# A two-layer decoder step on one core: the scan loop's selection mask moved to PSUM, and the second self-attention half and five folds placed elsewhere

## The reference

```python
x = x + mamba(layernorm(x))              # L0: projections, depthwise convolution, scan over 64 positions, gate, W_out
x = x + cross_attention(layernorm(x), ctx)   # L0: 16 heads of 128, keys and queries RMS-normed
x = x + two_expert_ffn(layernorm(x))     # L0: each row goes to the one expert its router picks
x = x + self_attention(layernorm(x))     # L1: 16 heads of 16, causal, ALiBi bias
x = x + cross_attention(layernorm(x), ctx, mask)  # L1: 16 query heads on 8 key heads
x = x + ternary_ffn(layernorm(x))        # L1: weights rounded to -1, 0, 1, rows to 8 bits

def step(state, inp):                    # the scan inside mamba
    dA = exp(dlt * A)
    state = dA * state + (dlt * u) * Bs
    y = einsum('bgdn,bgn->bgd', state, Cs)
```

## Time and profile before

| what | value |
|---|---|
| median of three runs | 927.2 us (924.82 to 931.52) |
| the profiled execution | 926.82 us, of which 924.9 us is the span from first to last instruction |
| scan loop, first to last step | about 40.2 to 273.8 us |
| second half of L1's self-attention, up to the folds | about 634.7 to 687.6 us |
| folds of L1 | 687.6 to 707.0 us |
| cross-attention and FFN of L1 | 707.0 to 924.9 us |

### The profile page before, as it was taken

One profiled execution on the slowest core, in us unless ns is written; L12 is line 12 of the kernel. 1 busy time (PEld: TensorE's weight loads), 2 busy tenths in 40 slices (PEclk: granted clock), 3 DMA queues, 4 the chain that ended last, 5 costly groups with the idle time before them and its releaser, 6 DMA issues.

```text
span 924.9 us, 12509 instructions
## 1 busy us (share of the span) xinstructions
PE 818.7 (89%) x5082; PEld 501.8 (54%) x5082; DVE 548.1 (59%) x666; ACT 434.1 (47%) x650; POOL 302.3 (33%) x147
## 2 busy tenths in 40 slices
PE   6687797977999889999999899997989799989976
PEld 2232333322445456566666676666677566667754
DVE  3799989899994232333433452437872534464686
ACT  3764666635524555555545312233554222232475
POOL 0089999899870000000001010102009990000000
PEclk9889999899999999999999999998989999999999
DMA  9666666776994100000000031415000000000001
GB/s 301 176 172 172 185 166 172 181 182 181 249 264 157 47 1 1 1 1 1 1 1 25 27 103 57 176 44 226 2 3 1 1 1 1 1 1 1 1 1 46
DMA packets 26377, 77.02 MB, mean 83 GB/s; under 512 B 3569, under 2 KB 10481, under 8 KB 25073
## 3 DMA queue, kind: packets, MB, share of 16 engines
q1 hardware_dynamic: 25552, 74.13, 27.8%
q0 software_dynamic: 768, 2.10, 0.6%
HBM read 68.75 MB, written 7.08 MB: 82 GB/s over the span
## 4 chain that ended last, share of the span: by engine, by line
PE 54%; DVE 13%; DMA 11%; ACT 10%; POOL 6%; issue 5%; SPq 0%; POOLq 0%; DVEq 0%; ACTq 0%
PE ps L1268 11%; PE ps L1184 9%; DMA region_b<-m_rows 5%; DMA region_c<-m_rows 4%; PE ps L1231 4%; PE ps L1367 4%; PE ps L1393 4%; POOL region_c L464 3%; PE ps L1256 3%; PE ps L1189 2%; POOL region_b L464 2%; DVE region_c L1827 2%; PE ps L1073 2%; PE ps L1025 2%; PE ps L1158 2%
## 5 line engine op out<-in xcount | busy, mean ns | idle before, releaser
L464 POOL TENSOR_TENSOR region_c<-region_c,region_b 128x1024 f32<-128x1024 f32 x42 | 101.1, 2415 | 51.6 <-DMA region_b<-m_rows 45.5
L1073 PE MATMUL ps<-region_c,ident 128*128 128x512 f32 x168 | 90.7, 669 | 18.9 <-POOL region_c L464 12.1
L1827 DVE TENSOR_TENSOR_SCAN region_c<-region_c,ps 128x1024 f32<-128x1024 f32 x43 | 97.8, 2283 | 2.0 <-ACT ps L635 0.8
L485 POOL DMA_INDIRECT f_in<-xn,f_row x8 | 8.0, 996 | 275.3 <-DVE f_row L1938 273.5
L1268 PE MATMUL ps<-region_c 128*128 128x256 f32 x384 | 90.4, 381 | 0.1
L1268 PEld LDWEIGHTS ps<-region_c 128*128 128x128 f32 x384 | 72.2, 190 | 24.8 <-issue 16.3
L1904 DVE COPY region_b<-ps 128x512 f32<-128x512 f32 x32 | 21.6, 689 | 84.9 <-PE ps L1242 84.8
L1822 DVE TENSOR_TENSOR ps<-ps,region_c 128x1024 f32<-128x1024 f32 x52 | 63.2, 1215 | 8.7 <-PE ps L1061 8.5
L1073 PEld LDWEIGHTS ps<-region_c,ident 128*128 128x128 f32 x168 | 33.7, 209 | 58.5 <-issue 34.5
L1184 PE MATMUL ps<-xnT,region_a 128*128 128x512 f32 x128 | 61.5, 602 | 0.8 <-ACT region_c L703 0.8
L1184 PE MATMUL ps<-xnT,region_c 128*128 128x512 f32 x128 | 58.6, 594 | 0.7 <-ACT region_c L731 0.7
(11 more groups left out here) (246 smaller groups left out, 1640.8 us busy)
## 6 DMA issues: line engine op xcount, KB each, us to landing
region_b<-m_rows SPq DMA_DIRECT2D x43, 512.0 KB, 5.1
region_c<-m_rows SPq DMA_DIRECT2D x21, 512.0 KB, 4.9
xn<-m_brows SPq DMA_DIRECT2D x12, 512.0 KB, 4.4
region_a<-in_x_wo SPq DMA_DIRECT2D x2, 2048.0 KB, 11.5
m_rows<-region_b SPq DMA_DIRECT2D x4, 512.0 KB, 5.7
region_a<-in_x_wq SPq DMA_DIRECT2D x8, 256.0 KB, 7.2
region_b<-in_f_fc SPq DMA_DIRECT2D x1, 2048.0 KB, 7.9
region_b<-in_f_proj SPq DMA_DIRECT2D x1, 2048.0 KB, 13.2
```

Of the source, the lines that this page charges most:

```text
L464: pool.tensor_tensor(m_hc[u % 3], m_h[u % 3], m_cb[u % 3], ALU.mult).then_inc(sem("m_hc"), 1)
L1073: last = pe.matmul(ps[:, 4 + c, :], ident[:, :], m_hc[u % 3][:, c * HALF:c * HALF + HALF], start=(n == 0), stop=(n == DST - 1))
L1827: dve.tensor_tensor_scan(m_h[u % 3], m_da[u % 3].rearrange("p b t -> p (b t)"), inputs(u), 0.0, ALU.mult, ALU.add).then_inc(sem("m_scan"), 1)
```

## The change

In the scan loop: the mask lies in PSUM (pair(6)) and is written one step later (n = 8), after c_rows has emptied pair(6) and, at k = 1, after the lags; convolve stands at n = 12 and waits for select_log, and convolved at n = 13. columns("C") stands at n = 2 and 3, c_rows at n = 4, columns("x") at 5 and 6, lags at 7 and 8. du has a buffer for each group (one of them is ctxT, so ctxT is loaded in group 3), and step_inputs stands one step sooner (n = 13). The first decay of a group stands ahead of channels. In L1: SP holds the 5 MB until gather(1) has landed; ln_scale, ln_turn of the second half stand ahead of shift 2 and scores 3; five folds (EARLY) stand among the self-attention; wvo and wqk lie over the weights they come from (in region A), and the FFN's buffers take their place; the output bias is added in two halves.

```diff
+            def decay(u): ...             # L629 as before, called at n > 0 or k == 0, and below
+        EARLY = [("wqk", 0), ("wvo", 0), ("wvo", 1), ("wvo", 2), ("wvo", 3)]
@@ SP
+            sp.wait_ge(sem("f_back"), 128)
-            load(wo1, io["x1_wo"], "ld_x1")
+            load(wo1, io["x1_wo"], "ld_t")
@@ GpSimd
-                if n == DST - 2 and k < NK - 1:
+                if n == DST - 3 and k < NK - 1:
                     step_inputs(k + 1)
@@ ScalarE, loop
-                act.activation(m_below, m_e, ACT.Relu, scale=-1.0, bias=thr_col)
+                act.wait_ge(sem("m_cT"), k + 1)
+                if k == 2:
+                    act.wait_ge(sem("m_xs"), 2)
+                act.activation(pair(6), m_e, ACT.Relu, scale=-1.0, bias=thr_col)
-                    if n == 6:
+                    if n == 4:
                         c_rows(k + 1)
-                    if n == 7:
+                    if n in (7, 8) and k == 1:
+                        lags(1, (2 * n - 14, 2 * n - 13))
+                    if n == 8:
                         step_below(k + 1)
-                    if n in (9, 10) and k == 1:
-                        lags(1, (2 * n - 18, 2 * n - 17))
-                    if n == 12:
+                    if n == 13:
                         convolved(k + 1)
                     if n == DST - 1:
+                        decay(u + 1)
                         channels(k + 1)
@@ ScalarE, self-attention
+            def early_folded(m):
+                act.wait_ge(sem("x1_fold"), m + 1)
+                act.activation(fold_out(1, *EARLY[m]), ps[:, 6 + m % 2, :], ACT.Copy).then_inc(sem("x1_folded"), 1)
-                act.wait_ge(sem("ld_t"), 48)      # weight_sum
+                act.wait_ge(sem("ld_t"), 64)
@@ TensorE
+                if n == 2 and k < NK - 1:
+                    pe.wait_ge(sem("m_ax"), k + 2)
+                    columns("C", k + 1, (0,))
                 if u >= 2:
                     add_state(u - 2)
-                    if n == 11:
-                        if k != 1:
-                            pe.wait_ge(sem("m_cT"), k + 2)
+                    if n == 12:
+                        pe.wait_ge(sem("m_sel"), k + 1)
                         convolve(k + 1)
+                if i == 7:
+                    for m in range(1, 5):
+                        early_fold(m)
+                    pe.wait_ge(sem("x1_folded"), 5)
@@ VectorE
-                dve.copy_predicated(m_ln, m_below.bitcast(mybir.dt.uint32), m_poly)
+                dve.copy_predicated(m_ln, pair(6).bitcast(mybir.dt.uint32), m_poly)
             a_sums(0)
-            a_shifts(2)
             ln_scale(3, 2)
             ln_scale(3, 3)
+            a_shifts(2)
```

More of the change, by code:

```diff
@@ L286, in head_order @@
             if layer == 1:
-                order += [(("wvo", i, 0), "act") for i in range(NH // 2)]
-                order += [(("wqk", i, 0), "act") for i in range(NH // 2)]
+                order += [(("wvo", i, 0), "act") for i in LATE_WVO]
+                order += [(("wqk", i, 0), "act") for i in LATE_WQK]
             for it in range(8 + 1):
@@ L333, in _ @@
             load(wo, io["x0_wo"], "ld_x0")
-            load(ctxT[:, :], io["ctxT"], "ld_x0")
             load(ctxn[:, :, :], io["ctxn"], "ld_x0")
@@ L622, in _, with decay @@
             exp_tables()
-            for u in range(NK * DST):
+            def decay(u):
                 k, n = u // DST, u % DST
@@ L630, in _ @@
                                scale=a_log[:, k, n:n + 1]).then_inc(sem("m_da"), 1)
+            for u in range(NK * DST):
+                k, n = u // DST, u % DST
+                if n or not k:
+                    decay(u)
                 if shared(u):
@@ L884, in _ @@
             ln_rstd(3, 3)
-            a_exps(2)
+            early_folded(0)
             ln_turned(3, 2)
             ln_turned(3, 3)
-            a_turned(2)
+            a_exps(2)
             projected(4)
             projected(5)
+            a_turned(2)
             a_exps(3)
@@ L896, in _ @@
             a_exps(4)
-            for i in range(5, 8 + 1):
+            a_exps(5)
+            a_turned(4)
+            weight_sum(1)
+            a_turned(5)
+            a_rows_turned(0)
+            early_folded(1)
+            early_folded(2)
+            a_exps(6)
+            early_folded(3)
+            early_folded(4)
+            weight_sum(2)
+            for i in range(7, 8 + 1):
                 if i < 8:
@@ L949, in beside_x1 @@
             def beside_x1(it, at):
-                if (it, at) == (-1, "fold 3"):
+                if (it, at) == (-1, "fold 7"):
                     a_rows_turned(1)
-                if (it, at) == (-1, "wqk 3"):
+                if (it, at) == (-1, "wqk 7"):
                     ln_rstd(4, 2)
@@ L1137, in _, with fold_wvo, fold_wqk @@
                     ln_turn(1, 1)
+            def fold_wvo(layer, i, b):
+                wv_h, wo_h = (wvT, wo) if layer == 0 else (wvT1, wo1)
+                for a in range(2):
+                    h = 2 * i + a
+                    last = pe.matmul(b[:, 256 * a:256 * a + 256], wv_h[:, h if layer == 0 else h // 2, :],
+                                     wo_h[:, h, :], start=True, stop=True)
+                return last
+            def fold_wqk(i, b):
+                for a in range(2):
+                    for k in range(KH):
+                        c = (2 * a + k) * 128
+                        last = pe.matmul(b[:, c:c + 128], wqT1[:, 2 * i + a, 128 * k:128 * k + 128],
+                                         wkT1[:, i, :], start=True, stop=True)
+                return last
             def cross(layer, beside):
@@ L1493, in a_context, with early_fold @@
                 last.then_inc(sem("a_ctx"), 1)
+            def early_fold(m):
+                what, i = EARLY[m]
+                if m >= 2:
+                    pe.wait_ge(sem("x1_folded"), m - 1)
+                if what == "wvo":
+                    pe.wait_ge(sem("ld_t"), 64)
+                    last = fold_wvo(1, i, ps[:, 6 + m % 2, :])
+                else:
+                    pe.wait_ge(sem("ld_x1"), 48)
+                    last = fold_wqk(i, ps[:, 6 + m % 2, :])
+                last.then_inc(sem("x1_fold"), 1)
             def a_turn_rows(half):
@@ L1586, in beside_x1 @@
             def beside_x1(it, at):
-                if (it, at) == (-1, "fold 3"):
+                if (it, at) == (-1, "fold 7"):
                     a_turn_rows(1)
-                if (it, at) == (-1, "fold 7"):
+                if (it, at) == (-1, "wqk 4"):
                     a_out(1)
@@ L1983, in _ @@
                 last = dve.tensor_scalar(qb_half[:, e, :], qkb[:, 0:2], parity[:, e:e + 1], None, ALU.mult)
-            last.then_inc(sem("a_qb"), 1)
+            after(last)
             after(dve.tensor_tensor(g_col, gq_col, gk_col, ALU.mult))
```

120 lines of the change are left out of this document (60 added, 60 removed).

## The result

The changed kernel takes 934.6 us (median of 20 runs, 930.5 to 939.9), the kernel before beside it 929.0. The ratio is 1.0066 (95% interval 1.0048 to 1.0084): slower, by about 6 us, which is clear of the noise and still within 1%. The forecast was 915.

What follows compares the result with a forecast made beforehand. VectorE and its waits bound the loop, an engine-changing chain the self-attention's second half, TensorE the folds. Loop -1.8 and part B -10.3 make -12.1 from 926.8, 914.7, said as 915 us; 8-in-10 range 909 to 920.

Steps and rivals of the forecast that it cites:

- the end of group 0: Scan loop boundary: u at about 94.5, step_inputs ends at 96.8, the next group's first multiply 1.3 us sooner.
- GpSimd's queue: Scan loop: step_inputs one step sooner makes GpSimd's last products of group 0 up to 1 us later.
- part A: The scan loop's edits: -0.4 + 0.1 - 1.5 = -1.8 us, ends +3 and -6.3.
- The copy: Selection's copy_predicated in the loop, mask in PSUM: 1.3 us instead of 3.39, 2.1 less three times.
- second rival: Loop: the copy stays at 3.4 us despite its PSUM mask; 919.2 to 919.6 us, chance 0.13.
- the third: Self-attention: gather(1) lands no sooner, its 7.0 us being its own; 918.6 us, chance 0.12.
- The lags: Loop, group 1: lags ahead of put 25 on ScalarE delay its scan, 3.3 us lost.
- The first rival: Loop gives all it could: copies 6.3 us whole, lags cost half; 4 to 5 more, 910 us, chance 0.20.
- the only rival that lost time: Slower than before: late loads hold the first mean if t_down lands after 665; chance 0.03.
- add_back: Self-attention's second half: no longer held by the gather, 3.44 us sooner.
- the transposes: Self-attention's second half: TensorE's transposes of the norm's xn at about 637.4, 6.5 us sooner.
- out_bias(1): Second half of the output bias, a GpSimd add: beside other work, costs nothing.

Runs made afterwards that it cites:

- chan: The changed kernel with the first decay of a group behind channels again; 0.9986 of the kernel before.
- inp14: The changed kernel with step_inputs one step later again (n = 14), the decay still ahead of channels; 0.9985 of the kernel before.
- mask02: part B plus, in the loop, only the mask in PSUM for groups 1 and 3, convolve and convolved one step later there; 0.9935 of the kernel before.
- lags_late: The kernel both, with columns x, lags and mask of group 2 as before the change; 0.9913 of the kernel before.
- part B: All of the change behind the scan loop (self-attention, folds, loads), with the loop of before; 0.9945 of the kernel before, 923.1 us beside 927.0.
- nohold: part B, but SP issues the 5 MB without waiting for gather(1); 0.9948 of the kernel before.
- bias: part B with the second half of out_bias held until ln_scale(4, 0) and (4, 1) are done; 0.9891 of the kernel before, 917.1 us.
- both: The changed kernel with decay behind channels and step_inputs at n = 14 again; 0.9921 of the kernel before.
- nofold0: part B without the early fold 0 of wqk, which is folded late with the others; 0.9951 of the kernel before.
- best: part B with the second half of out_bias later and the mask in PSUM for groups 1 and 3; 0.9862 of the kernel before, 915.8 us.
- exps_first: The kernel best with a_exps(6) ahead of the empties of early folds 1 and 2 on ScalarE; 0.9843 of the kernel before, 914.7 us.

## Why the prediction was wrong

**The step that failed is the end of group 0.** I had the ScalarE list there as put 14 at 90, then "decays 15 and 16 and channels (with its table load) behind it: 1.12, 1.12 and 2.4 us", u at 94.5, and du at 96.8. Put 14 came at 89.6, as forecast. But decay 16 is the first of the next group and reads its delta, which GpSimd ends at 93.0; it is no 1.12 us in a row but a wait of 1.38 until 93.06, with channels behind it. u came at 96.6 and du at 99.0. I had written that the decay ahead of channels "costs nothing either". chan shows what it cost: 7.4 us by the times, 9.2 at the three boundaries in the trace.

**GpSimd's queue at the same place.** I priced step_inputs one step sooner by when it would end, and its queue at "up to 1 us later". By my own 94.5, GpSimd would have idled from 93.0 to 94.5 with product 13 ready; by the true 96.6 it idled 3.6. On an engine that is busy for 212 of 234 us an idle time is given on to all that it feeds: state, add_state, put_b. inp14 shows 7.5 us by the times, 10.2 at the boundaries. The one edit makes u late and the other makes GpSimd wait for it, so the two share their cost: with both undone the boundaries give back 13.9 us (13.5 by the times), less than 9.2 and 10.2 together. The times alone can't tell a shared cost from an added one (7.4 and 7.5, each to some 3 us).

**Sums of part A.** The copy was right to 0.1 us (2.1 each), and 0.9 us of waiting ahead of the first one went too, though not by the copy (mask02 keeps most of it). The second rival (the copy stays at 3.4) is refuted, and so is the third (the gather lands no sooner): nothing waits for it ahead of add_back. The lags, forecast at 3.3, cost 3.3 in the trace and 3.2 by lags_late. Left out were columns("C") ahead of put_b(5), 2.2 us, and put 14 behind convolved, 0.9 twice. Forecast -1.8, measured +15.0: 13.4 of the 16.8 are the boundaries, against the forecast's small gains there. The first rival, that the loop gives all it could, is far off too; and its terms as written, 6.3 less half of 3.3, are 2.9 us more than my sum has and not 4 to 5. A result within 1% had a chance of 0.22, but as a mixture of gains that come out small; the only rival that lost time was put in the loads of part B, the last of which landed in 14.7 us and held nothing: I looked for the danger where a new wait was written in words, and not where an instruction moved past one that was there already.

**Part B was right in kind and wrong in size**: 4.75 us instead of 10.3. Right: add_back 3.6 sooner (nohold: 3.3), ln_scale 7.2 sooner, the loads not late, nothing changed behind the queries. Wrong: the transposes. I let them follow xn at once, but TensorE ends context 1 only at 652.5, 18.2 us after the first scores, because of a stop of 2.1 us within it (1.6 before), and then comes early fold 0; the 2.9 that the forecast 6.5 has too much fall on these two, though leaving out the fold gains nothing. It was wrong to let both gains run down the chain as one sum: in nohold the gather's 3.3 are lost at add_back and the transposes stand where they did. (The forecast's 6.2 at the folds has 0.45 more than the 5.75 ahead of context 5, with no term for it.) And out_bias(1), "beside, nothing": 4.1 us (bias). That last one is a mis-sized term of zero; rows 3 had shown what a GpSimd add does beside a VectorE instruction, and I used them for the copy alone. With bias mended, the first queries are 8.8 us sooner than before, near the forecast's 10.3.

**Open.** Step 62's 2.8 us: the product of step 58 waited 3.9 us, in a stretch with a DMA share of 1.04. ctxT is now loaded about there, but the same wait stands in bias, which has the loop of before and ctxT's load at its old place, and there it ends with a row of C:

```profile
258.85 2.34 POOL L468 TENSOR_TENSOR region_c<-region_c,region_b 128x1024 f32<-128x1024 f32 x1 [3.50 <-DMA region_c<-m_rows]
...
267.73 2.29 DVE L1874 TENSOR_TENSOR_SCAN region_c<-region_a,ps 128x1024 f32<-128x1024 f32 x1 [3.00 <-ACT ps L643]
```

It is missing in before, chan and both. So these 2.8 us of the 15.0 need not be the change's; why the row is late in some traces, no run separates. Why TensorE's clock fell in one trace and not in the other, after like waits, is open too.

## What to carry to other kernels

When an instruction is moved ahead of another in an engine's list, write down the time at which each of its inputs is ready, not only its duration: a decay of 1.1 us that reads another engine's late result made everything behind it wait. On an engine that is nearly full, put work whose input is late behind work that is ready, even if its own result then comes a little later. And side work that nobody waits for still needs a place: ask which instruction of the engine that shares its ports it will run beside.

## What the runs showed of the hardware

- copy_predicated of 128 x 1024 with the mask in PSUM takes 1.29 to 1.34 us beside GpSimd products, in every kernel that has it, and 3.31 to 3.41 with all operands in SBUF; with all in SBUF and no GpSimd product beside it, 1.35. So the destination in SBUF that must partly survive does not make it slow.
- TensorE's granted clock fell to its lower level after waits of some 2 us in some traces and not in others: after 1.86 us ahead of the transposes, four folds took 5.58 to 5.86 us in eight kernels and 3.79 in nofold0; where the wait was gone (bias, best, exps_first), they took 3.79. Wait and clock together cost about twice the wait's length here.
- The same projections took 3.70 us in part B, 5.42 without the fold of 2.1 us ahead of them (nofold0), and 6.28 with it but with a wait of 0.77 us ahead of the transposes (nohold). What an edit ahead of TensorE costs can lie in the clock of the stretch behind it, and with one trace each it can't be told from luck.
